# Attention and a mixture of experts on one core: the order of a half batch's score jobs, and the split of the query and key projections one slot later

## The reference

```python
def _L0_attn_ref(x, w_qkv, w_out):
    qkv = x @ w_qkv.T
    q, k, v = jnp.split(qkv, 3, axis=-1)            # 16 heads of 8
    att = jnp.einsum('bhqd,bhkd->bhqk', q, k) * SCALE
    allowed = (j <= i) & (j >= i - 128 + 1)
    att = jax.nn.softmax(jnp.where(allowed, att, -jnp.inf), axis=-1)
    out = jnp.einsum('bhqk,bhkd->bhqd', att, v)
    return out.transpose(0, 2, 1, 3).reshape(b, t, e) @ w_out.T

def _moe(x, router_w, w_in, b_in, w_out, b_out):
    probs = jax.nn.softmax(x @ router_w, axis=-1)
    top_p, top_e = jax.lax.top_k(probs, 2)
    # each token: sum over its two experts e of
    #   top_p * (gelu(x @ w_in[e] + b_in[e]) @ w_out[e] + b_out[e])

x = _layernorm(x + _L0_attn_ref(x, w_qkv, w_out))
x = _layernorm(x + _moe(x, router_w, w_in, b_in, w_out, b_out))
```

## Time and profile before

| | |
|---|---|
| median of three runs | 196.55 us |
| the profiled execution, its own time | 196.5 us |
| its span (first to last instruction) | 194.8 us |
| granted TensorE clock over the span | 0.994 |
| TensorE busy | 169.4 us, 87% |
| VectorE busy | 154.8 us, 79% |
| ScalarE busy | 114.6 us, 59% |
| GpSimd busy | 84.1 us, 43% |

### The profile page before, as it was taken

How to read it: one execution, slowest core, us unless ns; L and a number is a source line. 1 busy time by engine, 2 the same in 40 slices (tenths; PEclk the granted TensorE clock), 3 DMA queues, 4 the chain that set the end, 5 groups by cost and what they waited for, 6 DMA issues and landing times. The chain is left out here.

```text
span 194.8 us, 6184 instructions
## 1 busy us (share of the span) xinstructions
PE 169.4 (87%) x2450; PEld 121.5 (62%) x2460; DVE 154.8 (79%) x468; ACT 114.6 (59%) x216; POOL 84.1 (43%) x157
## 2 busy tenths in 40 slices
PE   7579887988989989889999899989999979999950
PEld 3354454655656656556656544558988869999950
DVE  6985959669598698697988999635798869898793
ACT  4542056687686766876857757564353784564720
POOL 7960006556563655746738366561043002603003
PEclk9999999999999999999999999999999999999997
DMA  5589594194780882955901000000000000020011
GB/s 142 148 232 222 168 242 132 53 212 125 158 226 11 176 206 72 214 160 110 218 13 57 2 8 0 3 0 0 5 0 0 3 27 27 0 59 0 3 53 54
DMA packets 23127, 17.25 MB, mean 89 GB/s; under 512 B 1827, under 2 KB 21179, under 8 KB 23099
## 3 DMA queue, kind: packets, MB, share of 16 engines
q1 hardware_dynamic: 23099, 16.87, 35.2%
HBM read 9.35 MB, written 7.34 MB: 86 GB/s over the span
## 5 line engine op out<-in xcount | busy, mean ns | idle before, releaser
L486 ACT ACTIVATE probs<-st 128x768 f32<-128x768 f32 x59 | 47.9, 811 | 23.8 <-PE st L1067 20.6
L443 POOL TENSOR_SCALAR_AFFINE_SELECT probs<-probs 128x1024 f32<-128x1024 f32 x32 | 35.1, 1097 | 57.4 <-ACT probs L486 57.3
L713 DVE TENSOR_REDUCE max_parts<-score_banks 128x2 f32<-128x384 f32 x64 | 32.6, 550 | 4.6 <-PE score_banks L1041 4.2
L594 ACT ACTIVATE hid<-score_banks,b_in_sb 128x512 f32<-128x512 f32 x32 | 21.9, 687 | 21.0 <-PE score_banks L1173 20.9
L716 DVE TENSOR_REDUCE max_parts<-score_banks 128x4 f32<-128x512 f32 x32 | 20.6, 686 | 13.6 <-PE score_banks L1041 13.6
L1067 PE MATMUL st<-stack 51*64 51x256 bf16 (+1 forms) x472 | 21.2, 254 | 6.2 <-ACT probs L486 5.7
L1030 PE MATMUL score_banks<-edges,ident_bf 64*64 64x256 bf16 (+1 forms) x192 | 19.0, 296 | 4.5 <-DVE max_parts L713 3.4
L1089 PE MATMUL o_bank<-probs,v 128*32 128x256 f32 x256 | 20.4, 391 | 0.0
L445 POOL TENSOR_SCALAR_AFFINE_SELECT probs<-probs 128x512 f32<-128x512 f32 x32 | 20.3, 634 | 0.0
L1067 PEld LDWEIGHTS st<-stack 51*64 51x64 bf16 (+1 forms) x472 | 8.6, 104 | 18.7 <-ACT probs L486 11.8
L860 DVE SCALAR_TENSOR_TENSOR x_rows<-st,gate,x_rows 128x128 f32<-128x128 f32 x64 | 18.1, 344 | 2.4 <-PE st L1187 2.0
(11 more groups left out here) (136 smaller groups left out, 331.2 us busy)
## 6 DMA issues: line engine op xcount, KB each, us to landing
stack<-scratch SPq DMA_DIRECT2D x28, 192.0 KB, 4.0
scratch<-parts SPq DMA_DIRECT2D x16, 192.0 KB, 4.0
scratch<-parts SPq DMA_DIRECT2D x24, 128.0 KB, 3.8
x_rows<-x SPq DMA_DIRECT2D x4, 256.0 KB, 5.6
out<-y_sb SPq DMA_DIRECT2D x8, 128.0 KB, 1.8
x_t_sb<-x_t SPq DMA_DIRECT2D x3, 256.0 KB, 4.8
w_in_sb<-w_in SPq DMA_DIRECT2D x1, 512.0 KB, 5.8
w_out_sb<-w_out SPq DMA_DIRECT2D x1, 512.0 KB, 7.9
```

Of the source, the lines that this page charges most:

```text
L443: pool.affine_select(out=own, in_=own, compare_op=ALU.is_ge, fill=0.0, base=0, pattern=[[0, 2], [0, 4], [1, P]], channel_multiplier=-1).th ...
L486: nc.scalar.activation(probs[g][:, :, two, :].rearrange("p k j c -> p j k c"), pair_banks(PAIRS * b + p)[:, :, 0:3 * P].rearrange("p j (k ...
L594: nc.scalar.activation(hid[e % 2][:, :], hid_bank[e % 2], ACT.Gelu_apprx_tanh, bias=b_in_sb[:, e:e + 1]).then_inc(gelu_done, 1)
L713: nc.vector.tensor_reduce(top[:, 1, r, pair:pair + 2], bank[:, 0:384].rearrange("p (h c) -> p h c", h=2), X_AXIS, ALU.max, negate=True).th ...
```

## The change

The table `SCORE_JOBS` gives the first two slots of each half batch to the second query tile and the third to the first tile. Batch 0 therefore needs only two picked pairs for its first job, and the waits on `even_stacked` and `odd_stacked` say so. `subtract_top` and `take_middle` move from slot 8b-13 to 8b-12, `take_low` and `write_parts` from 8b-12 to 8b-11. For batch 1 the write of the lower parts is taken out of `write_parts` and issued after `stack_first`. One pair of fillers in slot 1 goes. On TensorE and ScalarE the slots 64 to 74 are written out: the same pieces, some ahead of others, with one pair of fillers instead of eight, and with `first_layer(0, 0)` behind the last `turned_scores`.

```diff
-SCORE_JOBS = {0: (False, 0), 1: (True, 0), 2: (True, 2), 4: (False, 4), 5: (True, 4), 6: (True, 6)}
+SCORE_JOBS = {0: (True, 0), 1: (True, 2), 2: (False, 0), 4: (True, 4), 5: (True, 6), 6: (False, 4)}
 ...
@@ sync, write_parts
                 copies(b, 1, 1)
+                if b != 1:
+                    write_low(b)
+
+            def write_low(b):
+
                 sp.wait_ge(part_low, b + 1)
 ...
             sp.wait_ge(scratch_written[0], 80)
             stack_first()
+            write_low(1)
             sp.wait_ge(ones_ready, 2)
             stack(1)
 ...
-                b = batch_at(slot, PROJECT_QK + 2)
+                b = batch_at(slot, PROJECT_QK + 3)
                 if b is not None:
                     write_parts(b)
@@ scalar
-            for slot in range(LAST_S2 + 1):
+            for slot in range(LAST_S1 + 1):
 ...
-                for offset, piece in ((TURN_MAX, copy_max), (TURN_ATTN, copy_attention), (PROJECT_QK, take_top), (PROJECT_QK + 1, take_middle),
+                for offset, piece in ((TURN_MAX, copy_max), (TURN_ATTN, copy_attention), (PROJECT_QK, take_top), (PROJECT_QK + 2, take_middle),
                                       (VALUES, pad_v), (COPY_O, copy_output), (TURN_X1, copy_x1), (LOGITS, copy_logits)):
 ...
@@ tensor
-                if job == 0:
-                    pe.wait_ge(even_stacked, PICKED)
-                    pe.wait_ge(odd_stacked, PICKED)
+                if job < JOBS // 2:
+                    pe.wait_ge(even_stacked, pair + heads)
+                    pe.wait_ge(odd_stacked, pair + heads)
 ...
-                elif 0 < slot < S2:
+                elif 1 < slot < S2:
                     keep_warm(2)
 ...
-                b = batch_at(slot, PROJECT_QK + 1)
+                b = batch_at(slot, PROJECT_QK + 2)
                 if b is not None:
                     subtract_top(b)
-                if slot > LAST_S1 + 1 and slot < LAST_S2 - 1:
-                    keep_warm(2, hid_bank[0])
-                if slot == LAST_S2 - 1:
-                    pe.wait_ge(w_lo_done, 1)
-                    first_layer(0, 0)
-
-            weigh_values(B - 1, QUADS - 2)
+
+            late, last = B - 2, B - 1
+            turned_scores(late, 5)
+            turn_max(last)
+            turned_scores(late, 6)
+            weigh_values(late, 1)
+            turn_attention(late - 1)
+            turned_scores(late, 7)
+            weigh_values(late, 2)
+            project_out(late - 1)
+            keep_warm(2, hid_bank[0])
+            turned_scores(last, 0)
+            turned_scores(last, 1)
+            project_v(last)
+            weigh_values(late, 3)
+            turned_scores(last, 2)
+            turned_scores(last, 3)
+            turn_x1(late - 1)
+            turn_output(late)
+            turned_scores(last, 4)
+            route_logits(late - 1)
+            weigh_values(last, 0)
+            turned_scores(last, 5)
+            turn_attention(late)
+            turned_scores(last, 6)
+            weigh_values(last, 1)
+            project_out(late)
+            turned_scores(last, 7)
+            weigh_values(last, 2)
+            pe.wait_ge(w_lo_done, 1)
+            first_layer(0, 0)
             first_layer(0, 1)
 ...
```

More of the change, by code:

```diff
@@ L584, in _ @@
                         piece(b)
-                if slot == LAST_S1 + 3:
-                    route_exponentials(EARLY, 1)
+            late, last = B - 2, B - 1
+            exponentials(late, 5)
+            copy_max(last)
+            exponentials(late, 6)
+            copy_attention(late - 1)
+            exponentials(late, 7)
+            route_exponentials(EARLY, 1)
+            exponentials(last, 0)
+            exponentials(last, 1)
+            pad_v(last)
+            copy_output(late)
+            exponentials(last, 2)
+            exponentials(last, 3)
+            copy_x1(late - 1)
+            exponentials(last, 4)
+            copy_logits(late - 1)
+            exponentials(last, 5)
+            copy_attention(late)
+            exponentials(last, 6)
+            exponentials(last, 7)
             def gelu(c, e):
@@ L1276, in _ @@
                     weigh_values(*n)
-                b = batch_at(slot, PROJECT_QK + 1)
+                b = batch_at(slot, PROJECT_QK + 2)
                 if b is not None:
                     subtract_top(b)
-                if slot > LAST_S1 + 1 and slot < LAST_S2 - 1:
-                    keep_warm(2, hid_bank[0])
-                if slot == LAST_S2 - 1:
-                    pe.wait_ge(w_lo_done, 1)
-                    first_layer(0, 0)
-            weigh_values(B - 1, QUADS - 2)
+            late, last = B - 2, B - 1
+            turned_scores(late, 5)
[27 more added lines that the diff above has]
+            first_layer(0, 0)
             first_layer(0, 1)
             second_layer(0, 0)
-            weigh_values(B - 1, QUADS - 1)
+            weigh_values(last, 3)
             unit(0, 2)
```

## The result

The changed kernel takes 202.17 us (median of 4 runs, 200.12 to 203.11), the kernel before 196.56 beside it. The ratio is 1.0268, 95% interval 1.0183 to 1.0352: slower, as forecast, but by 5.6 us and not by 1.4, and outside the range of 196.2 to 199.4. The profiled execution took 203.11 us (span 201.4), the longest of the four.

A forecast was written before the change was run, and what follows sets the result against it. TensorE and VectorE were taken to set the pace in turns, with ScalarE inside the loop. The terms, -1.4 + 3.2 - 0.2 - 0.2 = +1.4 us on 196.5, gave 197.9 us, range 196.2 to 199.4.

The forecast's parts named there:

- Term 1: Start: first job needs two picked pairs, not four; slot 8 opens earlier, limited by batch 1's stack reads; -1.4 us.
- Term 2: Slots 12 to 47: ScalarE's middle copy waits for the later subtraction, delaying exponentials and openings in five batches; +3.2 us.
- What slot 30 gives back: Batches with a projection: TensorE's 0.73 us wait goes, as VectorE reduces slot 29's bank before writing the lower part.
- Term 3: Slots 48 to 63, without middle copy: waits shrink through VectorE's earlier reductions; -0.2 us.
- Term 4: Drain: fourteen fillers go, but VectorE, busy in unchanged order, sets the pace; -0.2 us.
- Rival E: Drain: TensorE's clock falls without the fillers, +8 us at most, put at +4; 202 us, chance 3%.
- Rival A: Batches: ScalarE's wait is hidden and VectorE's early reductions decide; faster, 194.4 us, chance 10%.
- rival D: Start: batch 1's reads land in 6.6 us, slot 8 opens at 23.9, 1.2 late; 200.5 us, chance 4%.
- rival C: Start gains its whole 2.3 us, slots 12 and 20 give back some 0.5; no change, 196.5 us, chance 12%.
- B: Drain: VectorE's long instructions shorten, no longer meeting GpSimd's; start gains its whole 2.3; faster, 195.7 us, chance 8%.

The follow-up runs named there:

- thin masks: Kernel before with the new drain and 4, 6 and 4 fillers, GpSimd's masks of the last two batches cut to one head of four: 195.05 us, ratio 0.9904.
- the kernel with the late copy: Kernel before with middle copy, lower part and writes one slot later, subtraction left in its old place: 198.42 us, ratio 1.0089.

## Why the prediction was wrong

Its direction and its main mechanism hold; what failed is the drain, and its clock above all. Step by step:

**Term 1, the start (-1.4): too large, and no gain is shown.** -0.85 by the openings without the new drain, -0.44 in the changed kernel's own profile. But each is one execution, and slot 11 opens anywhere from 26.36 to 27.14 us in the eleven kernels with the old start, from 25.67 to 26.85 in the five with the new one and no fall of the clock ahead of it. The wait for the stack is real: slot 8 opens at 22.40 behind 1.24 us for the reads, where I had 21.3. The four reads took SP longer to issue, 2.78 us in place of 1.77, as its queue shows:

```profile
13.78 0.43 SPq L275 DMA_DIRECT2D scratch<-parts  x1
16.03 2.78 SPq L303 DMA_DIRECT2D stack<-scratch  x4
```

I had put the first at 16.0, which is right, and the last at 17.3.

**Term 2, the middle copy (+3.2): right mechanism, a little large.** Slots 11 to 24 lost 1.25 (forecast 1.7), slots 24 to 48 1.20 (forecast 1.5). The order of the queue on ScalarE was read correctly; the subtraction starts 0.55 us behind the projection of v (54.79 to 55.34), where I allowed its whole 0.77. A batch took 13.8 us (41.31 for three), against 13.9. What slot 30 gives back I put down to the table, wrongly: the split alone, with the old table, loses the 0.73 us wait too (57.15 to the next opening at 58.74, 1.59 us; 1.96 before). In both kernels `turn_x1` then waits for VectorE's lower part, 0.54 us at 58.86 here.

**Term 3, the late batches (-0.2): wrong sign.** +0.45. I counted on VectorE's reductions being earlier, and so did not look at what the last job of a group leads to. In the changed kernel the mask of a first-tile job waits for VectorE later in the group, 0.60 us where the earlier trace rows have 0.40:

```profile
99.54 0.40 PE L1055 MATMUL score_banks<-edges,ident_bf 64*64 64x512 bf16 x2 [0.60 <-DVE max_parts L738]
```

The table is the cause: alone it costs 0.36, and the old one in these batches brings the wait back to 0.40 and 0.20 of the 0.35 us with it.

Terms 1 to 3 together: +2.05 against +1.6. Up to slot 64 the forecast is within 0.5 us of the undisturbed profile, in part by luck: term 2 came out 0.75 too large, terms 1 and 3 together 1.2 too low.

**Term 4, the drain (-0.2): the step that failed.** "They were not what the drain waited for" is true of the fillers and beside the point: they kept TensorE's clock. In the changed kernel this is nearly the whole of it: from slot 64 on it takes 86.54 us, 84.28 with fillers at the waits and 84.13 with the old drain, so the fall costs 2.3 and the order 0.15. By the medians the fillers bring 1.8 (202.17 to 200.41), with four runs each that overlap in part; on the old slots they bring 2.2 (199.92 to 197.74). The medians with fillers and with the old drain, 200.41 and 199.44, still differ by 1.0: ahead of slot 64 the profile with fillers has the two short falls and the other none, so this doesn't speak for a cost of the order.

The other premise, that VectorE "is busy 14.0 of 15.0 us" in an unchanged order, took its durations as fixed. They aren't: on the old slots the same order of pieces lengthens VectorE's chain by 0.99 us and costs 0.8 to 1.0, with GpSimd's masks beside other rows of it; with thin masks it gains 1.5. On the new slots this costs almost nothing. That the masks are the cause of the 0.8 to 1.0 is likely from these rows, and not shown apart from TensorE's own waits for them.

The sum, first for the profiled execution, 203.11 against 196.5: start -0.4, slots 11 to 24 +2.1, 24 to 48 +2.0, 48 to 64 +0.5, everything from slot 64 on +2.4 (86.54 in place of 84.12), together +6.6. In the two stretches with a short fall that is 0.9 and 0.8 more than the same slots took without one (+1.25 and +1.20). For the medians: 2.05 for terms 1 to 3, 2.7 for the new drain (199.44 to 202.17), which leaves 0.8 of the 5.6 for the short falls and what differs from run to run. No run isolates those.

**Rival E, the clock, was the one that came**, at 202 us. With 3% it was weighed far too low, and that its price came out is luck: I had +4 for the drain alone, where the fall cost 2.3; two short falls that I had nowhere made up the rest. (Its bound is also too low: some 10.6 busy us taking twice as long is +10.6 and not +8.) I had the rule before me: the Trainium skill, TensorE: Matmul & The Clock Gate, section HAM oscillation. I set it aside because every wait of up to 1.3 us before had left the clock alone. But my own step said that waits of some 2 us would stand in the drain, longer than any that the trace shows, with no fillers among them. The rows of before could not bear on that. The traces of the drain agree with the rule: in the changed kernel the clock falls at 125.56, just behind a wait of 1.80 us, and with the new drain alone at 121.69, inside the wait of 3.50. The short falls don't fit a rule of single long waits: at 74.4 none over 0.54 us stands in the 6 us ahead, at 33.70 in the kernel with the late copy none over 0.85. Rival A (ScalarE's wait hidden) is refuted by the ScalarE rows, rival D by slot 8, which opened at 22.40 and not at 23.9, rival C by the 1.25 us that slots 11 to 24 lost; B had the right resource (VectorE beside GpSimd) and, on the old slots, the wrong sign.

## What to carry to other kernels

Fillers can be work that the clock needs, as here: before taking them out, list the waits that will stand bare, and if one is longer than any wait that the trace shows at full clock, the clock is the first hypothesis and no side case. That covers the falls in the drain and not the short ones, which came behind waits of half a microsecond too. A duration on VectorE is a duration beside a certain neighbour; an order that only moves ScalarE or TensorE moves GpSimd too, and a long instruction of it onto VectorE's chain can cost more than the order gains. When a step is put one slot later, put what it waits for ahead of the long work of that slot: here that alone was worth 1.5 us of the split's 2.2.

## What the hardware showed unexpectedly

- The half clock came for 3.4, 6.8 or 10.2 us, in the profiles of seven of the seventeen kernels, while TensorE was busy most of the time (7.56 of 11.70 us ahead of it, 9.55 of 10.20 in it). The same instructions took 0.64 us at full and 1.08 at half clock.
- Equal kernels differ from run to run in mean granted clock and in time with it: the changed kernel ran 203.11 us at 0.947, 201.62 at 0.967 and 200.12 at 0.975; the kernel before ran 196.45 at 0.995 and 197.65 at 0.981.
- A VectorE instruction on 128x64 elements took 0.23 us alone and 1.15 beside a GpSimd mask, and a new order moved this from one row to another (1.07 at 118.26 before, 1.15 at 118.79 with the new drain); GpSimd's mask on 128x512 took 0.64 in the trace before and 1.62 beside VectorE's long subtraction. Both engines pay.
